# Gate logits of the second layer: four token tiles at a time, with the gate matrix as weights

## What is computed

```python
x = x + ga * _L1_attn_ref(h, L1_attn_Wq, L1_attn_Wk, L1_attn_Wv, L1_attn_Wfc)
h = _layernorm(x, axis=-1) * (1 + cb) + sb
# then, in the expert layer, xt = h as 4096 rows of 256:
logits = xt @ Wg            # Wg is 256 x 8: eight experts
probs = jax.nn.softmax(logits, axis=-1)
_, top_idx = jax.lax.top_k(probs.T, cap)
```

## Time and profile before

| | |
|---|---|
| median of 3 runs | 1049.5 us (1048.51 to 1049.79) |
| span of the profiled execution | 1045.7 us |
| instructions | 30362 |
| PE busy | 959.2 us, 92% |
| DVE busy | 690.6 us, 66% |
| ACT busy | 496.8 us, 48% |
| POOL busy | 377.1 us, 36% |
| mean granted TensorE clock | 0.969 of full speed |

### The profile page before, as it was taken

The page is one execution under the profiler, slowest core; times in us unless marked ns, Lnnn a source line. Parts: engine busy times, 40 slices in busy tenths (PEclk is TensorE's granted clock), DMA queues, the critical chain, the costliest instruction groups (busy, mean ns, idle before and its releaser), DMA issues. The chain is left out here.

```text
span 1045.7 us, 30362 instructions
## 1 busy us (share of the span) xinstructions
PE 959.2 (92%) x11177; PEld 823.6 (79%) x11178; DVE 690.6 (66%) x1747; ACT 496.8 (48%) x1343; POOL 377.1 (36%) x330
## 2 busy tenths in 40 slices
PE   6899999889999999999987999999767888999996
PEld 3466666879999999999965778888666878899995
DVE  3478877855777777777412688889985776344442
ACT  3556665404454554554446777777552440322221
POOL 0134335521223223222213455555561101455552
PEclk9999999999999999999998899999868999999998
DMA  9885581294232222221055657766421620444441
GB/s 338 216 331 122 126 269 41 97 386 115 85 102 79 87 97 85 89 92 71 8 107 92 115 124 150 154 134 128 99 68 57 266 108 22 151 134 140 134 136 35
DMA packets 133025, 135.59 MB, mean 130 GB/s; under 512 B 73884, under 2 KB 122142, under 8 KB 130740
## 3 DMA queue, kind: packets, MB, share of 16 engines
q1 hardware_dynamic: 121684, 90.80, 31.5%
q0 software_dynamic: 11232, 43.27, 13.0%
HBM read 96.21 MB, written 44.77 MB: 135 GB/s over the span
## 5 line engine op out<-in xcount | busy, mean ns | idle before, releaser
L1151 PE MATMUL psall<-rows 128*128 128x128 f32 x1872 | 224.8, 277 | 1.6 <-issue 1.1
L1151 PEld LDWEIGHTS psall<-rows 128*128 128x128 f32 x1872 | 219.6, 194 | 3.1 <-issue 1.3
L1114 POOL DMA_INDIRECT x<-ffn_rows,tok_i x78 | 82.6, 1059 | 171.8 <-DVE tok_i L999 69.9
L1165 PE MATMUL psall<-whi,rows 128*128 x624 | 141.0, 379 | 0.0
L1244 DVE COPY rows<-wlo 128x2048 f32 (+2 forms) x78 | 74.5, 955 | 95.8 <-PE psall L1151 85.2
L1165 PEld LDWEIGHTS psall<-whi,rows 128*128 128x128 f32 x624 | 115.7, 190 | 14.1
L1119 POOL DMA_INDIRECT attn_rows<-rows,tok_i x39 | 41.7, 1070 | 183.9 <-DVE rows L1276 183.9
L1504 DVE STREAM_TRANSPOSE whi<-whi 32x512 f32<-32x512 f32 x128 | 89.7, 701 | 9.1 <-POOL whi L1467 7.7
L1584 ACT ACTIVATE whi<-psall 32x512 f32<-32x512 f32 x128 | 75.3, 588 | 30.8 <-PE psall L1713 27.3
L280 PE MATMUL psall<-cst 128*128 128x128 f32 x714 | 88.4, 280 | 0.5 <-PEq L1387 0.5
L1306 ACT ACTIVATE rows<-psall,vs 128x128 f32<-128x128 f32 x312 | 85.0, 383 | 4.4 <-PE psall L1151 2.1
(11 more groups left out here) (250 smaller groups left out, 1731.3 us busy)
## 6 DMA issues: line engine op xcount, KB each, us to landing
ffn_rows<-mod_rows SPq DMA_DIRECT2D x2, 4096.0 KB
wlo<-in_W SPq DMA_DIRECT2D x2, 4096.0 KB, 17.5
whi<-in_w SPq DMA_DIRECT2D x5, 1024.0 KB
whi<-mod_rows SPq DMA_DIRECT2D x4, 1024.0 KB, 15.0
ffn_rows<-rows SPq DMA_DIRECT2D x8, 512.0 KB
ffn_rows<-x SPq DMA_DIRECT2D x8, 512.0 KB
wlo<-attn_rows SPq DMA_DIRECT2D x32, 128.0 KB, 3.4
v_turn<-wlo SPq DMA_DIRECT2D x32, 128.0 KB, 2.6
```

The lines of the kernel that those rows point to most:

```text
L1114: eng.indirect_dma_start(xin[j % DEEP], None, src_d, bass.IndirectOffsetOnAxis(tok_i[:, j:j + 1].bitcast(U32), 0), bounds_check=T, oob_is_ ...
L1151: last = eng.matmul(b_up[t.par][f // 4][:, (f % 4) * P:(f % 4 + 1) * P], w_now[:, c, f * P:(f + 1) * P], inT[t.par][:, c * P:(c + 1) * P], ...
L1165: last = eng.matmul(b_dn[t.par][:, 0:D], hidT[t.par][:, f * P:(f + 1) * P], w_down[:, bass.ds(e, 1), f, :].rearrange("p o n -> p (o n)"), ...
```

## The change

`logits` for tiles 0 to 27 is replaced by two stages. `group_logits` runs once in four steps, at the fourth tile of a group: the gate matrix is the weight matrix, 128 x 8, in column strip k for tile k, and the four kept tiles `h1T[0..3]` stream through, so that eight matmuls give the logits of 512 tokens, experts down and tokens across, in `b_lgT` of bank 6. ACT copies the four strips to `affT` (`keep_turned_logits`). One step later `turn_logits` transposes `affT` into `b_lgB` of bank 6, as the first work of PE in that step, and ACT copies the 4 x 8 columns of it to `key3` (`keep_group_logits`, between `shift_h` and `keep_v`). `keep_h1T` now keeps four tiles. The last four tiles keep the old form. The semaphores `lg` and `key` count twice for a group, and the waits follow them.

```diff
--- before.py
+++ after.py
@@ -1338,7 +1338,7 @@
         hT = [cw(C * S).rearrange("p (c n) -> p c n", c=C) for _ in range(2)]
         n1 = [cw(D) for _ in range(4)]
         vrow = [cw(D) for _ in range(2)]
-        h1T = [cw(D) for _ in range(2 + TB)]
+        h1T = [cw(D) for _ in range(TB)]
         mod3 = [cw(3 * D).rearrange("p (j d) -> p j d", d=D) for _ in range(2)]
         xr = [cw(TB * D).rearrange("p (k d) -> p k d", d=D) for _ in range(3)]
         mx1 = [cw(GR) for _ in range(2)]
@@ -1354,7 +1354,8 @@
         b_qk = [ps[4], ps[5]]
         b_T = ps[6][:, 0:D]
         b_h = [bank[:, 0:D] for bank in (ps[6], ps[6], ps[4], ps[5], ps[1], ps[2])]
-        b_lg = [bank[:, D:D + E] for bank in (ps[6], ps[6], ps[4], ps[5], ps[1], ps[2])]
+        b_lg = [bank[:, D:D + E] for bank in (ps[4], ps[5], ps[1], ps[2])]
+        b_lgT, b_lgB = ps[6][:, D:D + P], ps[6][:, D + P:D + 2 * P]
         b_pv, b_v = ps[7][:, 0:D], ps[7][:, D:2 * D]
 
         v_d = nc.dram_tensor("v_turn", [NT, P, D], F32).ap()
@@ -1598,20 +1599,33 @@
 
                 def keep_h1T(t):
                     eng.wait_ge(c_["tH"], t + 1)
-                    if t < FIRST_LAST:
-                        wait_some(eng, c_["lg"], t - 1)
-                    eng.activation(one_of(h1T, t), one_of(b_h, t), ACT.Copy).then_inc(c_["h1T"], 1)
+                    wait_some(eng, c_["lg"], 2 * (t // TB) - 1)
+                    eng.activation(h1T[t % TB], one_of(b_h, t), ACT.Copy).then_inc(c_["h1T"], 1)
+
+                def keep_turned_logits(t):
+                    if t % TB == TB - 1:
+                        eng.wait_ge(c_["lg"], 2 * (t // TB) + 1)
+                        for k in range(TB):
+                            last = eng.activation(affT[QD * k:QD * k + E, :], b_lgT[QD * k:QD * k + E, :], ACT.Copy)
+                        last.then_inc(c_["key"], 1)
+
+                def keep_group_logits(t):
+                    b = t // TB
+                    if t % TB == TB - 1:
+                        eng.wait_ge(c_["lg"], 2 * b + 2)
+                        eng.activation(key3[:, b * TB:(b + 1) * TB, :], b_lgB.rearrange("p (k n) -> p k n", k=TB)[:, :, 0:E], ACT.Copy
+                                       ).then_inc(c_["key"], 1)
 
                 def keep_logits(t):
-                    eng.wait_ge(c_["lg"], t + 1)
-                    eng.activation(key3[:, t, :], one_of(b_lg, t), ACT.Copy).then_inc(c_["key"], 1)
-                tile_steps([(LAG_MX, compact((0, 1), False)), (LAG_N, shift_h), (LAG_V, keep_v), (LAG_EX, exps), (LAG_MX, compact((2, 3), True)),
-                            (LAG_H, keep_h1T), (LAG_QK, keep_qk), (LAG_PV, keep_oT), (LAG_H, keep_logits), (LAG_X, rstd2)],
+                    eng.wait_ge(c_["lg"], 2 * (FIRST_LAST // TB) + t - FIRST_LAST + 1)
+                    eng.activation(key3[:, t, :], b_lg[t - FIRST_LAST], ACT.Copy)
+                tile_steps([(LAG_MX, compact((0, 1), False)), (LAG_N, shift_h), (LAG_H + 1, keep_group_logits), (LAG_V, keep_v), (LAG_EX, exps), (LAG_MX, compact((2, 3), True)),
+                            (LAG_H, keep_h1T), (LAG_QK, keep_qk), (LAG_PV, keep_oT), (LAG_H, keep_turned_logits), (LAG_X, rstd2)],
                            [(LAG_MX, compact((0, 1, 2, 3), True)), (LAG_N, shift_h), (LAG_V, keep_v), (LAG_EX, exps), (LAG_QK, keep_qk),
-                            (LAG_X, rstd2), (LAG_H, keep_h1T), (LAG_PV, keep_oT), (LAG_H, keep_logits)])
+                            (LAG_X, rstd2), (LAG_H, keep_h1T), (LAG_PV, keep_oT), (LAG_H, keep_turned_logits)])
                 keep_h1T(FIRST_LAST - 1)
                 rstd2(FIRST_LAST)
-                keep_logits(FIRST_LAST - 1)
+                keep_turned_logits(FIRST_LAST - 1)
                 rstd2(FIRST_LAST + 1)
                 for t in LAST:
                     keep_h1T(t)
@@ -1619,6 +1633,8 @@
                         rstd2(t + 2)
                     if t > FIRST_LAST:
                         keep_logits(t - 1)
+                    else:
+                        keep_group_logits(t - 1)
                 keep_logits(NT - 1)
 
             @block.tensor
@@ -1632,7 +1648,8 @@
                 def turn_n(t):
                     eng.wait_ge(s_n1[t % 4], 16 * (t // 4 + 1))
                     wait_some(eng, c_["hT"], t)
-                    wait_some(eng, c_["key"], done_by(t, LAG_N, LAG_H, 1))
+                    wait_some(eng, c_["h1T"], done_by(t, LAG_N, LAG_H, 1))
+                    wait_some(eng, c_["key"], 2 * (done_by(t, LAG_N, LAG_H, 1) // TB) - 1)
                     for c in range(C):
                         last = eng.transpose(b_T[:, c * P:(c + 1) * P], n1[t % 4][:, c * P:(c + 1) * P], ident)
                     last.then_inc(c_["nT"], 1)
@@ -1672,7 +1689,8 @@
                     eng.wait_ge(c_["h"], t + 1)
                     wait_some(eng, c_["hT"], done_by(t, LAG_H, LAG_N))
                     if t < FIRST_LAST:
-                        wait_some(eng, c_["key"], t)
+                        wait_some(eng, c_["h1T"], t)
+                        wait_some(eng, c_["key"], 2 * (t // TB))
                     for c in range(C):
                         last = eng.transpose(one_of(b_h, t)[:, c * P:(c + 1) * P], one_of(h1, t)[:, c * P:(c + 1) * P], ident)
                     last.then_inc(c_["tH"], 1)
@@ -1693,12 +1711,24 @@
                                                   e8[:, :, half * HH:(half + 1) * HH], start=half == 0, stop=half == 1)
                     last.then_inc(c_["pv"], 1)
 
+                def group_logits(t):
+                    if t % TB == TB - 1:
+                        eng.wait_ge(c_["h1T"], t + 1)
+                        wait_some(eng, c_["key"], 2 * (t // TB) - 1)
+                        for c in range(C):
+                            for k in range(TB):
+                                last = eng.matmul(b_lgT[QD * k:QD * k + E, :], wg[:, c, :], h1T[k][:, c * P:(c + 1) * P], start=c == 0, stop=c == C - 1)
+                        last.then_inc(c_["lg"], 1)
+
+                def turn_logits(t):
+                    if t % TB == TB - 1:
+                        eng.wait_ge(c_["key"], 2 * (t // TB) + 1)
+                        eng.transpose(b_lgB, affT, ident).then_inc(c_["lg"], 1)
+
                 def logits(t):
                     eng.wait_ge(c_["h1T"], t + 1)
-                    if t < FIRST_LAST:
-                        wait_some(eng, c_["key"], t)
                     for c in range(C):
-                        last = eng.matmul(one_of(b_lg, t), one_of(h1T, t)[:, c * P:(c + 1) * P], wg[:, c, :], start=c == 0, stop=c == C - 1)
+                        last = eng.matmul(b_lg[t - FIRST_LAST], h1T[t % TB][:, c * P:(c + 1) * P], wg[:, c, :], start=c == 0, stop=c == C - 1)
                     last.then_inc(c_["lg"], 1)
 
                 def scores(t):
@@ -1719,19 +1749,21 @@
                     if t >= NT - 2:
                         eng.wait_ge(c_["ve"], NT)
                         hold_clock(eng, 12, b_unread)
-                tile_steps([(LAG_N, turn_n), (LAG_V, values), (LAG_QK, queries_keys), (LAG_H, turn_h), (LAG_PV, hold_last), (LAG_PV, weigh),
-                            (LAG_H, logits), (LAG_S, scores)],
+                tile_steps([(LAG_H + 1, turn_logits), (LAG_N, turn_n), (LAG_V, values), (LAG_QK, queries_keys), (LAG_H, turn_h), (LAG_PV, hold_last),
+                            (LAG_PV, weigh), (LAG_H, group_logits), (LAG_S, scores)],
                            [(LAG_N, turn_n), (LAG_V, values), (LAG_QK, queries_keys), (LAG_Y, project), (LAG_H, turn_h), (LAG_PV, hold_last),
-                            (LAG_PV, weigh), (LAG_H, logits), (LAG_S, scores)])
+                            (LAG_PV, weigh), (LAG_S, scores)])
                 hold_clock(eng, 6, b_unread)
                 turn_h(FIRST_LAST - 1)
                 hold_clock(eng, 3, b_unread)
-                logits(FIRST_LAST - 1)
+                group_logits(FIRST_LAST - 1)
                 hold_clock(eng, 12, b_unread)
                 for t in LAST:
                     turn_h(t)
                     if t > FIRST_LAST:
                         logits(t - 1)
+                    else:
+                        turn_logits(t - 1)
                     hold_clock(eng, 3, b_unread)
                 logits(NT - 1)
 
```

## The result

The changed kernel takes 1052.2 us (median of 20 executions, 1046.3 to 1057.4). The kernel before, timed beside it, takes 1048.6 us (20 executions, 1045.3 to 1051.2). The ratio is 1.0035, 95% interval 1.0021 to 1.0048: slower by about a third of a per cent. The forecast was 1052.6 us. A second timing of the same kernel gave 1.0010 (0.9995 to 1.0026), a third 1.0031 (1.0017 to 1.0045).

The account below looks back on a forecast made before the run. A DVE-PE-ACT-POOL loop of 29.46 us, not PE, was taken as the bound. Loop 0, clock +3.9, late steps -0.8 make +3.1 us on 1049.5: 1052.6 us; 8-in-10 range 1047.5 to 1056.5 us.

Parts of the forecast that it names:

- PE is not what the loop waits for: Middle steps: a 29.46 us loop through DVE, PE scores, ACT, POOL and DVE; PE's saved 1.4 us a group counts 0.
- The rival of 1039.6 us: PE is the bound after all: 28 tiles save 9.9 us, giving 1039.6 us; chance 0.05.
- PE's prices: Per group of four steps, logits on PE cost 0.75 us in place of 2.16 us, saving 1.4 us.
- ACT's copies: Four copies, 1.08 us a group, delay compact and mask 0.45 us against 0.40 us slack; counted 0, upper bound 2.7 us.
- the copies' rival: ACT's copies become the bound: DVE waits 0.3 to 0.8 us a group, 3.0 us in all, 1051.7 us; chance 0.12.
- PE's wait: Before the project step's scores, PE idles about 1.9 us, where it idled 0.65 us.
- Falls of the clock: After PE's wait, the granted clock falls in three of the four project steps 22, 26, 30 and 34.
- Price of a fall: Each fall costs the loop 1.1 us if short, 2.5 us at most, mean 1.3; three cost 3.9 us.
- Late steps: From step 38, where PE enters the chain, removed logits gain 0.8 us, between 0 and 2.5; tail 0.
- The signs that I named: Profile after: L1490 idle about 2.1 us, loops 29.5 us, PE idle 1.7 to 2.0 us, falls giving 30.5 to 32 us loops.
- signs of being wrong: Loops shorter than 29.4 us, clock 1.00 throughout, or DVE's norm2 waiting for `rstd2` in the step after the copies.
- the clock's theory: Project steps: the loss is the granted clock falling after PE's longer wait; +3.9 us in the forecast, chance 0.48.

Follow-up runs that it names:

- e4: The kernel before with four added unread ACT copies of 8 x 128 from PSUM at each group's fourth tile, PE's logits kept: 1047.52 us, ratio 1.0000.
- r2: The changed kernel again, nothing altered, one more profiled execution: 1051.7 us.
- r3: The changed kernel again, nothing altered, another profiled execution: 1049.2 us.
- r4: The changed kernel timed again, nothing altered, beside new runs of the kernel before: 1052.11 us, ratio 1.0031.
- e5: The changed kernel with five unread matmuls in PE's wait of project steps 22 to 38 and one ACT copy in place of four: 1047.85 us, ratio 0.9990.
- r1: The changed kernel timed again, nothing altered, beside the kernel before: 1049.25 us, ratio 1.0010.
- e1: The changed kernel with five unread matmuls between weigh and scores in project steps 22 to 38: 1047.98 us, ratio 1.0000.
- b1: The kernel before, unchanged, run again as one of the kernels with a profile: 1048.93 us, ratio 0.9996.
- e7: The changed kernel with one ACT copy and five unread matmuls in PE's wait of project steps 18 to 38: 1049.54 us, ratio 0.9996.
- e8: The changed kernel with one ACT copy, unread matmuls in project steps 18 to 38 and also before late turn_h and project stages: 1045.71 us, ratio 0.9976.
- e2: The changed kernel with one ACT copy of 128 x 128 in place of the four of 8 x 128: 1046.23 us, ratio 0.9998.
- e3: The kernel before without the logits matmuls of tiles 2, 6, ..., 26, lengthening PE's wait, no ACT work added: 1047.03 us, ratio 1.0004.

## Why the prediction was right, and where its terms were off

**PE is not what the loop waits for: right.** PE's busy time fell by 1.15 us of 29, and no loop up to step 34 became shorter; the maxima still wait 2.07 us once in four steps, as in the earlier trace rows. The rival of 1039.6 us is out.

**PE's prices: right.** From `group_logits` to the scores it took 701.93 - 701.37 = 0.56 us (0.75 in step 27, where nothing behind it moved by that), and the transpose, of 0.33 us, 0.21 or so up to the next record; I had 0.75 us for both from the earlier trace rows. The Trainium skill, "TensorEngine Tiling (Array Packing)", Performance Considerations, gives a factor of four for this swap. The trace agrees about PE: eight strip matmuls for four tiles take 0.62 us, where one tile took 0.61. It is worth nothing to this loop.

**ACT's copies: a term that was mis-sized.** I had the compact 0.35 us late, the copy to `key` 0.1, and 0.40 us of slack of the mask, so 0 to 0.1 us a loop. Measured is 0.32. Against the maxima of the same step the compact starts at 673.96 - 672.50 = 1.46 us, before at 673.83 - 672.97 = 0.86: 0.60 us late, not 0.35. The copies themselves were as worked out, 1.11 us for 1.08, started when the old one did. The fault is in the next line: I had the copies end at 673.8, `rstd2` at 674.3 and the compact start at 674.2, as if it could pass an instruction in front of it. `rstd2` is two instructions, and the compact began 0.55 us after its first (673.41 to 673.96). The copy to `key` then added 0.08, as said, and the mask was 0.68 us late. The 0.45 us that I gave as a bound was none, since it took the same misplaced start; it holds only because the slack was not subtracted from it. The three loops from step 22 to 34, where it can be read, give 1.0 us, five such loops would give 1.6, and so much of the copies' rival is true. The compact is 0.60 us late here and only 0.50 with the same copies in e4; why stays open. The same page of the Trainium skill, section PSUM Bottleneck, warns that the copy out of PSUM may become the bound; ACT was not (22.68 us of 29 busy), but in its queue the copies held back what DVE waited for.

**PE's wait: right in kind, 1.30 us and not 1.9.** I had added the 0.54 us of the logits of the step before. PE does not come earlier by it, since the projection now waits for ACT's compact (L1585), which stands behind `rstd2` in ACT's queue, and this waits for DVE's sums. In steps 22, 26, 30 and 34 that wait was 0.32, 0.16, 0.33 and 0.92 us; in the kernel before the profile marks none. In step 26:
```profile
659.44 3.74 PE L1685 MATMUL psall<-rows,whi 32*128 32x256 f32 x64 [0.16 <-ACT whi L1585]
```
The projection starts 664.37 - 659.44 = 4.93 us before the gate product, and 664.83 - 660.01 = 4.82 in the kernel before: of the 0.54 us PE keeps 0.1. The 1.30 us are 0.65 of before, 0.54 of the missing logits, and 0.1.

**Falls of the clock: right in kind, fewer than three.** In five profiled executions of the changed kernel 7 of 20 waits in steps 22 to 34 were followed by a fall, 1.4 an execution. With the wait filled there were none in 16 waits (four kernels). In the other profiled kernels there were 4 in 20: one of eight in the kernel before, two of four with one copy, one of four with the skipped logits and none of four with the added copies. I took three of four from step 18's fall. That step is more regular than the others: in twelve profiled executions without filling there, six had PE waiting 1.25 to 1.32 us and fell, six had it waiting 0.60 and did not. So a wait of 1.3 us was followed by a fall each time there and about one time in three in the later steps, and what else decides is open. Over all these unfilled project steps, 16 of 34 waits of 1.1 to 1.32 us were followed by a fall and one of 18 waits of 0.43 to 0.76 us.

**Price of a fall: 1.41 us on a loop of 29.77, predicted 1.1 to 1.3.** Over the loop of before it is 1.73 us, since the copies hold back `rstd2` just then. The loop from step 34 shows no clean price: 29.43 and 29.48 us with a fall, 28.70, 28.78 and 30.28 without, the last with the longer low stretch near 748 us.

**Late steps: right.** I counted 0.8 us, between 0 and 2.5. The loop from step 38 took 30.3 us on average over five executions, 31.3 over the two of before, and the next 24.7 against 25.0: 1.3 us gained. The loop from step 34, which I had not counted among the late ones, gained another 0.6 (29.33 against 29.92). The gate product of step 42 waits less for the projection:
```profile
783.48 1.42 DVE L1515 TENSOR_TENSOR whi<-psall,wlo 128x256 f32<-128x256 f32 x4 [1.51 <-PE psall L1685]
```
against, in the kernel before,
```profile
784.49 1.42 DVE L1514 TENSOR_TENSOR whi<-psall,wlo 128x256 f32<-128x256 f32 x4 [2.16 <-PE psall L1668]
```
In the tail I counted 0; from the last gate product to the router's maxima it took 13.17 us for 12.97: 0.2 us lost to the extra copy and transpose.

**The signs that I named.** The 2.07 us at the maxima came. The loops without a fall were 29.78 us and not 29.5, and PE's wait 1.30 and not 1.7 to 2.0. The profile after has one fall in the middle steps, in the loop from 723.94 us, which took only 29.43 us; loops of 31.2 us after a fall came in r2, r3 and r4. And of the signs of being wrong one came in part: norm2 waited 1.32 us for `rstd2` in the step after the copies, though only behind a fall.

**The sum.** From the table of loops, the mean of the five executions of the changed kernel less the mean of the two of before: copies 3 x 0.32 = 1.0; falls in steps 22 to 30, one an execution at 1.4, less 0.5 x 1.2 = 0.6 in the kernel before, +0.8; from step 34 on -1.9; tail +0.2: +0.1 us in all. I had +3.1, as +3.9 for falls and -0.8. All executions of the changed kernel average 1051.4 us, and the weighted mean of the three timed differences (+3.6, +0.8, +2.9 us) is +2.7 us. So the sign and size of the forecast are right, and the way is right in kind: a slightly longer loop and falls of the clock against a gain in the late steps. That 1052.6 comes so near to 1052.2 us is luck. The term of the falls was five times what the profiled executions show, the copies stood at nothing, the late gain was put too low, and a second timing of the same kernel gave +0.8 us.

**What stays open.** The profiled executions alone do not show the loss: from step 18 to 46 the five of the changed kernel take 204.7 us on average, and the two of before, one of them with a fall, 204.75. They are not fair samples: the five are shorter (1048.6 us on average) than the rest, and the second of before, at 1052.25 us, is the longest of its 12. What the longer executions of the changed kernel do in the loops was not seen. Executions also differ where the change does nothing: the gate product of step 18 started between 603.3 and 605.7 us in the five, and at 605.7 and 607.3 in the two. From the last gate product to the end of the span it took 236.3 to 237.6 us in both kernels.

The granted clock says something. Every execution comes with its mean clock, over the whole of it, and in most kernels the longer executions have the lower clock: in the changed kernel 4 to 7 us go with 0.01 of clock (correlations -0.71 to -0.80), in the kernel before 4.5 to 7; in e5 hardly any such relation is seen (-0.26). A part of this clock is that of steps ahead of the change: from 526 to 603 us it was 0.89 in r2 and 0.93 in the other four. The means:

```
kernel                     executions   mean us   mean clock   beside before
after                          20       1052.06     0.9698         +3.6
after again, r1                12       1049.76     0.9726         +0.8
after again, r4                12       1052.12     0.9713         +2.9
before (beside e1 to e4)       35       1047.75     0.9714
before (beside r1 and e5)      23       1048.94     0.9713
before (beside r4, b1, e7, e8) 35       1049.18     0.9717
with filling, e1               12       1047.66     0.9749         -0.1
with one copy, e2              12       1046.42     0.9722         -1.3
both, e5                       12       1048.05     0.9756         -0.9
both, and step 18, e7          12       1049.32     0.9767         +0.1
filled late too, e8            12       1046.89     0.9820         -2.3
wait alone, e3                 12       1047.32     0.9705         -0.4
copies alone, e4               12       1047.62     0.9716         -0.1
before, again, b1              12       1049.06     0.9714         -0.1
```
Filling raised the clock, and no filled kernel shows the loss, as the clock's theory says. But r4 has the clock of before and still costs 2.9 us, more than the copies' 1.6 at most. And the single copy gave back more (3 us by its ratio and 4 by the means, against the changed kernel's +2.7, the two not timed beside each other) than its 1.6 us and its falls, cheaper by a quarter of a us each, come to. So three things are shown: the copies make a loop 0.32 us longer, a fall after steps 22 to 30 makes it 1.2 to 1.4 us longer, and with both mended (e5, e7) the kernel is faster than the changed one timed beside it. That these two effects are the whole of the timed 2.7 us is not shown, nor how the loss divides between them. The wait alone (e3, though with a single fall in its profile) and the copies alone (e4) cost nothing that could be measured.

## What to carry to other kernels

A saving on the engine with the highest busy share is worth nothing to a loop that closes over another one; read the loop from one fixed instruction to its next turn before counting. Look at what the saving leaves behind: a longer idle time of PE can cost clock, work put in to fill it must fit the wait of each step in which it stands (it did in steps 22 to 34, and held the scores back by 0.65 and 1.02 us in steps 18 and 38), and a small copy in another engine's queue delays whatever stands behind it, here a 0.3 us operation for which the bound engine waits. Copy all partitions at once, unused ones too, and judge the clock by several profiles, since one profile shows one draw of it.

## What the runs showed of the hardware

One thing that I had not expected, and one that is not as it seemed. A fall of the granted clock to its lower level (0.57 to 0.62 over 4 us, so 1.2 GHz for most of it) followed a wait of only 0.72 us in the kernel before, and did not follow 13 of 20 waits of 1.3 us in the changed one: the same program at the same place differs from execution to execution. And added matmuls, which do nothing, did not reliably make the time steadier: the standard deviation is 0.9 us in e5, but 1.7 in e1 and e7 and 3.1 in e8, against 1.5 to 2.1 us in the kernel before and 1.9 to 2.7 in the changed one.
